# Gated y and B turned by VectorE's block transposes and a trip through DRAM instead of on TensorE

## The reference, cut to what matters

```python
proj = x @ W_in.T                       # gives xp, z, B_ssm, C_ssm, dt_low
dt = softplus(dt_low @ dt_W.T + dt_b)
scores = einsum('bcihn,bcjhn->bcijh', Cc, Bc) * Lm * dtc[:, :, None, :, :]
y_intra = einsum('bcijh,bcjhp->bcihp', scores, xc)
chunk_state = einsum('bckhn,bckhp->bchnp', Bc, wx)
...
y = (y_intra + y_cross).reshape(B, S, H, P) + xp * D_param[None, None, :, None]
y = y / rms * norm_w
y = y * silu(z)
return y @ W_out.T
```

## Time and profile before

| what | before |
|---|---|
| median of 3 runs | 2918.6 us (2917.18 to 2920.0) |
| profiled execution, its own time | 2926.86 us |
| span of the profiled execution | 2925.1 us |
| busy: PE, DVE, ACT, POOL | 95%, 70%, 59%, 50% |
| mean granted TensorE clock | 0.988 of full |

### The profile page before, as it was taken

The page is one execution under the profiler, slowest core; times in us unless marked ns, Lnnn a source line. Parts: engine busy times, 40 slices in busy tenths (PEclk is TensorE's granted clock), DMA queues, the critical chain, the costliest instruction groups (busy, mean ns, idle before and its releaser), DMA issues.

```text
span 2925.1 us, 135112 instructions
## 1 busy us (share of the span) xinstructions
PE 2769.8 (95%) x59836; PEld 2237.4 (76%) x59836; DVE 2053.4 (70%) x2871; ACT 1715.0 (59%) x3424; POOL 1463.4 (50%) x2319
## 2 busy tenths in 40 slices
PE   8999999999999999999999999999677787899998
PEld 7888888888888888888888888887566676455554
DVE  6777777777777777777777777777444443788998
ACT  5666566566666666656656656665333333666674
POOL 4666666666667667666666666666110000111111
PEclk9999999999999999999999999999899998899999
DMA  4222222222222222222222222222644443578776
GB/s 154 78 73 69 74 78 76 73 78 77 72 79 74 72 82 73 73 77 74 75 75 78 74 72 79 76 73 58 215 132 136 110 123 119 178 222 269 234 228 195
DMA packets 262711, 316.37 MB, mean 108 GB/s; under 512 B 28000, under 2 KB 184032, under 8 KB 260464
## 3 DMA queue, kind: packets, MB, share of 16 engines
q1 hardware_dynamic: 252176, 297.55, 33.7%
q10 hardware_dynamic: 9952, 10.17, 1.1%
HBM read 194.31 MB, written 113.31 MB: 105 GB/s over the span
## 4 chain that ended last, share of the span: by engine, by line
PE 89%; DVE 4%; issue 4%; DMA 1%; SPq 1%; POOL 1%; ACT 0%; ACTq 0%; DVEq 0%; POOLq 0%
PE a_proj L991 41%; PE a_mix L991 12%; PE s_ps L1714 6%; PE g_pick_ps L1465 6%; PE a_scan L1105 5%; PE s_ps L1735 4%; DVE g_picked L1394 3%; PE s_ps L1730 3%; PE a_scan L1082 3%; PE a_scan L1069 2%; PE g_acc_ps L1489 2%; PE a_mix L1057 2%; PE a_misc L1049 1%; PE a_misc L1123 1%; DMA part_dram<-res 1%
## 5 line engine op out<-in xcount | busy, mean ns | idle before, releaser
L991 PE MATMUL a_proj<-wdh,xTh 128*128 128x512 f32 x1024 | 421.2, 411 | 5.5 <-issue 3.7
L991 PE MATMUL a_proj<-wdh,xTl 128*128 128x512 f32 x1024 | 402.4, 393 | 0.3 <-issue 0.3
L991 PE MATMUL a_proj<-wdl,xTh 128*128 128x512 f32 x1024 | 400.0, 391 | 1.7 <-issue 1.7
L823 DVE COPY_PREDICATED scan_in<-mask,a_scan 64x512 f32<-64x512 uint32 x512 | 382.4, 747 | 16.1
L1671 ACT COPY s_stage<-s_ps 128x1024 f32<-128x1024 f32 x256 | 279.2, 1147 | 150.9 <-PE s_ps L1714 142.4
L464 POOL TENSOR_TENSOR dx<-xs,d_row 64x512 f32<-64x512 f32 x256 | 331.4, 1294 | 15.1
L472 POOL TENSOR_TENSOR yv<-yt,dx 128x512 f32<-128x512 f32 x128 | 189.0, 1476 | 293.2 <-DVE yt L863 293.2
L639 ACT ACTIVATE scan_in<-CT,hsel 64x128 f32<-64x128 f32 x1024 | 326.2, 388 | 4.8
L603 ACT ACTIVATE raw<-a_proj,rs 128x272 f32<-128x272 f32 x128 | 62.5, 488 | 427.4 <-PE a_proj L991 427.4
L1394 DVE COPY g_picked<-g_pick_ps 128x1024 f32<-128x1024 f32 x128 | 156.7, 1224 | 218.4 <-PE g_pick_ps L1465 218.4
L1691 DVE STREAM_TRANSPOSE s_turned<-s_stage 128x2048 f32<-128x2048 f32 x128 | 294.4, 2302 | 9.8 <-ACT s_stage L1671 9.8
(11 more groups left out here) (152 smaller groups left out, 7275.3 us busy)
## 6 DMA issues: line engine op xcount, KB each, us to landing
x<-in_x_dram SPq DMA_DIRECT2D x128, 256.0 KB, 2.7
xn_dram<-xn SPq DMA_DIRECT2D x128, 256.0 KB, 2.4
part_dram<-res SPq DMA_DIRECT2D x128, 256.0 KB, 2.5
g_xn<-xn_dram SPq DMA_DIRECT2D x512, 64.0 KB, 2.3
s_part<-part_dram SPq DMA_DIRECT2D x128, 256.0 KB, 4.1
out_dram<-s_out SPq DMA_DIRECT2D x128, 256.0 KB, 3.8
xr<-in_xT_dram SPq DMA_DIRECT2D x126, 256.0 KB, 2.9
s_inner<-inner_dram SPq DMA_DIRECT2D x32, 512.0 KB, 4.1
```

The lines of the kernel that those rows point to most:

```text
L823: nc.vector.copy_predicated(dst, mask[rows_, :].unsqueeze(1).unsqueeze(1).to_broadcast([CH, 4, 2, CH]), src).then_inc(mt_cp, 1)
L991: last = nc.tensor.matmul(out, lhs[a], rhs[c], start=(k == 0 and n == 0), stop=(k == nk - 1 and n == 2))
```

## The change

TensorE no longer turns y or B, but for the very last tile of y. DVE transposes 32x32 blocks of gated y (turn_yz) and of scaled B (turn_b) into the buffer blocks; SP stores them to DRAM and loads them back with the blocks in their new places, in four loads for four groups of 32 partitions. One store with its four loads, "even", carries y of tile n1 and B of both tiles of block s (512 KB each way); the other, "odd", carries y of tile n2+1 (256 KB each way). copy_bT, hi_yz and lo_yz read the loaded tiles in SBUF in place of PSUM. ygh and ygl get a second buffer, and the memory for all of it comes from a smaller scratch of the DMA program. Orders on ACT and the older issues of SP are kept; SP's new issues stand between them.

```diff
+    def features(n):
+        return (odd[:] if n % 2 else even[:, :, 0:KI, :]).rearrange("p b k t -> p k b t")
+    def even_part(s):
+        return slice(0 if valid(s - 1) else KI, 2 * KI if valid(s) else KI)
+    def odd_steps(s):
+        return max(0, s - 1)
...
+        def store_even(s):
+            part = even_part(s)
+            cols = slice(GRP * part.start, GRP * part.stop)
+            if valid(s):
+                sync.wait_ge(b_turned, s + 1)
+            if valid(s - 1):
+                sync.wait_ge(y_turned, 2 * s - 1)
+            sync.dma_start(keep["even"][s, :, :, cols], blocks[:, :, part, :].rearrange("p g k t -> p g (k t)")).then_inc(even_out, 16)
+        def load_even(s):
+            part = even_part(s)
+            cols = slice(GRP * part.start, GRP * part.stop)
+            sync.wait_ge(even_out, 16 * (s + 1))
+            wait(sync, yg_lo, 2 * s - 3)
+            wait(sync, bT_cp, 2 * s)
+            for g in range(4):
+                sync.dma_start(even[GRP * g:GRP * g + GRP, :, part, :].rearrange("p b k t -> p b (k t)"),
+                               even_rows[s, g][:, :, cols]).then_inc(even_in, 16)
+        def store_odd(s):
+            sync.wait_ge(y_turned, 2 * s - 2)
+            sync.dma_start(keep["odd"][s], blocks[:, :, 0:KI, :].rearrange("p g k t -> p g (k t)")).then_inc(odd_out, 16)
+        def load_odd(s):
+            sync.wait_ge(odd_out, 16 * odd_steps(s))
+            wait(sync, yg_lo, 2 * s - 4)
+            for g in range(4):
+                sync.dma_start(odd[GRP * g:GRP * g + GRP, :, :, :].rearrange("p b k t -> p b (k t)"),
+                               odd_rows[s, g]).then_inc(odd_in, 16)
         def load_x(n):
             sync.dma_start(x[:, n % (2 * STB), :], x_dram[n]).then_inc(x_in[n % (2 * STB)], 16)
                     store_xn(t, t)
             if valid(s):
                 load_rsb(s)
+            if valid(s - 2) and s < NST + 1:
+                store_odd(s)
+                load_odd(s)
             if valid(s + 1):
                 store_xn(2 * (s + 1), 0)
...
                 load_x(2 * (s + 2))
+            if s < NST + 1:
+                store_even(s)
             if valid(s + 1):
                 store_xn(2 * (s + 1) + 1, 1)
+            if s < NST + 1:
+                load_even(s)
             if valid(s - 2):
                 store_part(s - 2, 1)
...
         def copy_bT(n):
-            act.wait_ge(bT_ps, n + 1)
-            nc.scalar.copy(BT[:], misc[:, 0:HALF].rearrange("p (f t) -> p f t", f=2)).then_inc(bT_cp, 1)
+            act.wait_ge(even_in, 64 * (n // 2 + 1))
+            wait(act, sc_ps, 4 * n)
+            part = KI + 2 * (n % 2)
+            nc.scalar.copy(BT[:].rearrange("p f (b t) -> p b f t", t=GRP), even[:, :, part:part + 2, :]).then_inc(bT_cp, 1)
         def copy_x(n):
...
         def hi_yz(n):
-            act.wait_ge(yzT_ps, n + 1)
             if n == NT - 1:
+                act.wait_ge(yzT_ps, 1)
                 for i in range(2):
                     act.wait_ge(xn_out[i], 16 * NST)
-            nc.scalar.copy(gated(n)[0], turned(n)[:].rearrange("p (k t) -> p k t", k=KI)).then_inc(yg_hi, 1)
+                nc.scalar.copy(gated(n)[0], turned(n)[:].rearrange("p (k t) -> p k t", k=KI)).then_inc(yg_hi, 1)
+            else:
+                act.wait_ge((even_in, odd_in)[n % 2], 64 * (n // 2 + 2 - n % 2))
+                wait(act, o_ps, n - 1)
+                nc.scalar.copy(gated(n)[0].rearrange("p k (b t) -> p k b t", t=GRP), features(n)).then_inc(yg_hi, 1)
...
-            wait(dve, yzT_ps, n - 1)
+            wait(dve, y_turned, n - 1)
             nc.vector.tensor_tensor(yz[:, n % 2, :], yv[:], sz[:, n % 4, :], ALU.mult).then_inc(yz_cp, 1)
+        def turn_yz(n):
+            s = n // 2 + 1 + n % 2
+            wait(dve, even_out, 16 * s)
+            wait(dve, odd_out, 16 * odd_steps(s - n % 2))
+            dve.wait_ge(yz_cp, n + 1)
+            nc.vector.transpose(blocks[:, :, 0:KI, :], yz[:, n % 2, :].rearrange("p (k g l) -> p g k l", k=KI, g=4)).then_inc(y_turned, 1)
+        def turn_b(s):
+            wait(dve, even_out, 16 * s)
+            wait(dve, odd_out, 16 * odd_steps(s))
+            dve.wait_ge(scaled, 2 * s + 2)
+            for i in range(2):
+                last = nc.vector.transpose(blocks[:, :, KI + 2 * i:KI + 2 * i + 2, :],
+                                           raw[:, (2 * s + i) % 4, C_B:C_DT].rearrange("p (f g l) -> p g f l", f=2, g=4))
+            last.then_inc(b_turned, 1)
         def lo_yz(n):
             dve.wait_ge(yg_hi, n + 1)
             hi, lo = gated(n)
...
-            nc.vector.tensor_tensor(lo, turned(n)[:].rearrange("p (k t) -> p k t", k=KI), hi.bitcast(F32),
-                                    ALU.subtract).then_inc(yg_lo, 1)
+            if n == NT - 1:
+                nc.vector.tensor_tensor(lo, turned(n)[:].rearrange("p (k t) -> p k t", k=KI), hi.bitcast(F32),
+                                        ALU.subtract).then_inc(yg_lo, 1)
+            else:
+                hi, lo = [y.rearrange("p k (b t) -> p k b t", t=GRP) for y in (hi, lo)]
+                nc.vector.tensor_tensor(lo, features(n), hi.bitcast(F32), ALU.subtract).then_inc(yg_lo, 1)
         def residual(n, i):
             dve.wait_ge(o_ps, n + 1)
...
             if valid(s - 2):
+                if s < NST + 1:
+                    turn_yz(n2 + 1)
...
                 expand_c(n1 + 1)
+            if valid(s - 1):
                 gate(n1)
+                turn_yz(n1)
+            if valid(s):
+                turn_b(s)
             if valid(s + 1):
                 stats(2 * (s + 1) + 1)
                 finish_stats(2 * (s + 1) + 1)
...
+            pe.wait_ge(scaled, n + 1)
             pe.wait_ge(x_cp, n + 1)
             wait(pe, yt_cp, n)
             wait(pe, mt_cp, 4 * n)
...
             pe.wait_ge(yg_lo, n + 1)
+            if n < NT - 1:
+                wait(pe, res_cp, n)
             for k in range(KI):
                 last = split_mm(turned(n)[:], [y[:, k, :] for y in gated(n)], [w[:, k, :] for w in wo], k, KI)
...
                 project_bdt(n0 + 1)
-            if valid(s - 1):
-                transpose_b(n1)
             if valid(s):
                 project_x(n0)
-            if valid(s - 2):
-                transpose_yz(n2)
             if valid(s - 1):
                 chunk_states(n1)
                 scores(n1)
             if valid(s):
                 project_z(n0)
-            if valid(s - 1):
-                transpose_b(n1 + 1)
             if s == NST:
                 pe.wait_ge(z_cp, NT)
...
             if s == NST + 1:
                 gather["pick"](pe, 0, 1)
-            if valid(s - 2) and s < NST + 1:
...
+        even=nc.dram_tensor("even_dram", [NST + 1, P, 4, 2 * KI * GRP], F32, kind="Internal").ap(),
+        odd=nc.dram_tensor("odd_dram", [NST + 1, P, 4, KI * GRP], F32, kind="Internal").ap(),
...
-    nc = bacc.Bacc("TRN2", target_bir_lowering=False, num_devices=1)
+    nc = bacc.Bacc("TRN2", target_bir_lowering=False, num_devices=1, dynamic_dma_scratch_size=1024)
```

34 lines of the change are left out of this document (18 added, 16 removed).

## The result

The changed kernel takes 2930.26 us (median of 6 runs, 2926.18 to 2938.61); the kernel before, in the same rounds, 2919.26 (2916.31 to 2920.63). The ratio is 1.0045, 95% interval 1.0029 to 1.0061: slower by half a per cent, where a gain of 1.4% was forecast. The profiled execution has a span of 2936.8 us and a time of its own of 2938.61, the longest of the six; that of the kernel before was 8 us over its median too, so the two traces may be held against each other.

What follows compares the result with a forecast made beforehand. The prediction took PE to bound the loop. From the profiled 2926.9 us it took 62 for the loop and added 20 for the end: 2884.9, or 2877 against the median; own range 2862 to 2891, 8-in-10 range 2842 to 2925.

Steps and rivals of the forecast that it cites:

- What PE gives back: PE's transposes in a stage: removing those of y and B frees 1.48 us, 93 us over some 63 stages.
- What is late next: PE's sums wait 0.5 us for POOL's dA, held up by lo_yz; stage 30.4 us, gain 62 us over 63 stages.
- DVE: DVE in a stage: block transposes add 1.9 us, 24.9 busy of 30.4; full, but not setting the stage.
- the bound of 30.7: DVE in the loop: if each block transpose took 0.75 us, the stage would be 30.7 us.
- The round trip: Stores and loads of turned y and B: hidden in the loop, with 6 us to spare for even, 4.7 for odd.
- The end: End of the phase: turn_yz on DVE waits for the odd store behind the weight loads; a loss of 20 us.
- 2926.9 - 62 + 20: Whole kernel: profiled time less the loop's gain plus the end's loss, 2884.9, or 2876.6 against the median.
- PE alone: Rival for the loop: PE stays the only bound, POOL costs nothing; 2846 us, chance 0.18.
- the port in full: Rival at POOL: lo_yz holds it for its whole 0.65 us; gain 46 us, time 2893, chance 0.12.
- slower: Rival at POOL: block transposes hold it too, dA 1.35 us late; gain 8 us, time 2931, chance 0.14.
- the end did cost: Judges the rival that the phase's end costs nothing, store_odd getting past the weights: 2857 us, chance 0.09.
- the loads weren't late: Judges the rival that loads come over 6 us late, each us beyond costing 63 us; chance 0.05.

Runs made afterwards that it cites:

- e9: Changed kernel with lo_yz reading its second operand from PSUM instead of SBUF, low part of y left out: 2929.68 us, 1.003 of the kernel before.
- e14: Kernel before with POOL's first spread_c product of a stage issued twice, so that dA comes later: 2959.38 us, 1.0105 of the kernel before.
- e2: Changed kernel with POOL's inv_std of the next x tile moved behind step_sizes, so that dA comes earlier: 2895.68 us, 0.9918 of the kernel before.
- e1: Changed kernel with stage 64's turned-y stores and loads and result stores issued ahead of the weight loads: 2920.8 us, 0.9994 of the kernel before.
- e10: Changed kernel with the even x tile's store and the result store held back on SP until project_x(n0+1) is done: 2928.86 us, 1.0029 of the kernel before.
- e13: Changed kernel with inv_std behind step_sizes and POOL's first spread_c product of a stage issued twice: 2958.94 us, 1.0103 of the kernel before.
- e8: Changed kernel with transpose_b put back, so PE turns B and only y goes the new way: 2918.51 us, 0.9957 of the kernel before.
- e7: Kernel before with only B turned the new way, y still turned by PE: 2896.8 us, 0.9891 of the kernel before.
- e5: Changed kernel with stage 64's stores and loads ahead of the weight loads and inv_std behind step_sizes: 2884.48 us, 0.9852 of the kernel before.
- e15: Changed kernel with inv_std behind step_sizes and the first half's store_xn and store_part behind SP's wait for the second project_x: 2903.88 us, 0.9918.
- e4: Kernel before with the change's stores and loads added, read by nobody, none in stage 64; transposes stay on PE: 2926.7 us, 1.0019.
- e6: Kernel before with only its two result stores of stage 64 issued ahead of the weight loads: 2920.95 us, 0.9988 of the kernel before.
- e3: Changed kernel with 12 matmuls of 4 columns a stage added in the places of the removed transposes: 3005.79 us, 1.0286 of the kernel before.
- e12: Kernel before with only B turned the new way, stage 64's result stores ahead of the weight loads, inv_std behind step_sizes: 2872.66 us, 0.9842.
- e11: Kernel before with only POOL's inv_std moved behind step_sizes: 0.9983 of the kernel before, 5 us.

## Why the prediction was wrong, point by point

The time was forecast at 2877 and came out at 2930, above its range.

*What PE gives back*: 1.48 us a stage forecast, 1.32 measured. B's pairs gave 0.22 each. Of 0.52 for a set of y's, 0.44 came: the 0.31 from the last matmul to chunk_states holds 0.08 that 0.23 between plain matmuls didn't show. I took the distance from the first transpose to the next work, and forgot that the next work's first start behind a large matmul has a price of its own.

*What is late next*: right in mechanism, and in size partly by luck. The wait at the sums was forecast at 0.5 us and is 0.58 in the mean of 62. The hold lies where it was put, on the row ahead of dA, and is 0.32 us for 0.4; but mv also comes from DVE 0.22 us later, which the forecast had at nothing. The Trainium skill, SBUF — State Buffer, section "Who interferes with whom", has a DVE instruction with two SBUF inputs exclude one of GpSimd that reads SBUF. The trace agrees for lo_yz (nm 502 ns, 193 in e9). Not foreseen were 0.10 us between the start of the sums and project_x (1.49 for 1.39; e14, which only adds a wait, has 1.49 too) and 0.08 a stage in the mean for chunk_states. 1.32 - 0.58 - 0.10 - 0.08 = 0.56, and the usual stage came down by 0.47; the last 0.1 is not accounted for. It is some 30 us over the loop for 62.

*DVE*: turn_yz takes 0.71 us (0.6 taken, bound 0.75) and turn_b 0.73 (0.7). "DVE is full but doesn't set the stage" held for the change in that PE waits for POOL's dA and not for DVE, though a part of dA's lateness is DVE's, as just said. It did set it in e2, at 30.72, so the bound of 30.7 that I gave for slow transposes became the floor as soon as dA was early.

*The round trip*: hidden in the loop, as worked out. The page's DMA part has the even store at 2.6 us and part_dram's at 3.3 (2.5 before):

```profile
part_dram<-res SPq DMA_DIRECT2D x128, 256.0 KB, 3.3
...
even_dram<-blocks SPq DMA_DIRECT2D x63, 512.0 KB, 2.6
```

No wait of ACT for even or odd is among those between 300 and 1900 us.

*The end*: a loss of 20 us forecast, 16.3 measured; turn_yz waited 23.40 us for odd_dram's store. Right.

*The step that failed* is in the sum: "2926.9 - 62 + 20". Both of its sides missed. The 62 us are 35 too many: the usual stage gives 0.47 us and not 0.98, 27 us over 58 stages, by the pieces just listed. And it has no term for PE's pauses, which the earlier trace rows hide, since the stretch with 596.6 of 600 us busy has only two of them, 1.84 and 0.92 us: in the stages from the sixth on the excess grew by 22 us, and the first stages lost 2. The end was 4 too dear, and what lies behind it 1 shorter. 35 + 22 + 2 - 4 - 1 is the 54 us between forecast and profiled time. The mis-sized gain alone would have left the time at some 2908, still faster and in the range; the pauses made it slower.

*What lengthens the pauses.* Each pause follows an instruction packet by 2.2 to 3.3 us, with busy DMA engines or idle ones. Over all traces the length goes with how long dA is ready before PE starts the sums, rather than with whether PE waits for it. These are the pauses of over 0.8 us between 300 and 1900 us in which PE ran dry in the scan behind the sums or just after it (within 2.1 us of the sums' start). Where PE waits for dA, 0.05 us from its end to the sums' start remain:

```text
end of dA ahead of the sums' start, us        number of pauses and their length, us
0.05, PE waits    after                       7    2.11 to 2.86
                  e1                          7    2.12 to 2.88
                  e9                          7    1.83 to 2.99
                  e10                         7    1.61 to 2.60
                  e14                         3    2.30 to 3.00
                  e13, six stages             6    1.77 to 2.44
0.05 to 0.15      e8, PE barely waits         8    1.01 to 2.88
0.38, no wait     e7                          3    2.70 to 2.77
0.66 to 0.86      e2, e5, e15                21    1.29 to 2.05
0.85              e13, the seventh stage      1    1.48
0.91 to 0.92      before, e4, e6             18    0.82 to 2.19
1.36              e3                          3    0.86 to 1.71
1.65              e12                         2    0.97
2.2               e11                         3    1.03 to 1.28
```

Moving dA changes them in both directions: moving inv_std shortens them in the changed kernel (e2), in the kernel before (e11) and with B alone (e12 against e7, which differ otherwise only in SP's orders of stage 64); the doubled product lengthens them (e13, e14). Moving the stores does little where PE waits (e10) and nothing in e15. So a dA that comes close to its use costs twice where PE waits for it, in each stage and once more in each seventh, and in e7 it costs pauses alone. Not shown: why PE's packet comes later when dA is late just ahead of the scan; when a packet is asked for stands in no view. e8 has both long and short pauses with dA at the same distance, so this isn't all. That the long ones come every seventh stage now goes with the number of PE's instructions in a stage, since e2, with the same stream, has its pauses at the same places; how the packets' borders line up with the stages wasn't tried. e4's traffic, with no wait for dA, made the three pauses 0.24 us shorter, 0.46 longer and 0.23 longer, which is no more than e6 shows without it, so what the traffic does there is open.

*Rivals*: "PE alone" was wrong by POOL and DVE; "the port in full" came nearest with 0.73 us of stage gained for 0.47; "slower" gave the right time by the wrong way, since in the stage shown dA is later by 0.46 us against project_bdt, 0.29 of it in POOL's operations and 0.17 because DVE is later, and not by the 1.25 of that rival; the end did cost; the loads weren't late.

## What to carry to other kernels

Before counting an engine's freed instructions as time, look for the pauses of that engine without a cause: sum the stages' excess over the median stage, and treat it as a term of its own, that grew here from 17 to 39 us when an input of the work just ahead of a burst of small instructions came 0.9 us later against PE, and that can grow without any wait to show for it. Take off the bound engine only as much as the next two engines in line can follow; here a third of the edit (B, four of the twelve transposes) gave as short a usual stage as all of it, with none of the end's loss. And when work is added to a queue, its last iterations need an order of their own ahead of the next phase's bulk loads.

## What the runs showed of the hardware

Pauses of PE of 2 to 3 us were mostly followed by a granted clock of 0.50 for three to five us (33 of 48 in the 17 traces between 300 and 1900 us), and those of 0.8 to 1.5 us never (0 of 56); of those between, 7 of 32 were. The length alone doesn't decide: after 2.58 us at 1548.81 in the changed kernel the clock stayed full (excess 2.48), after 1.76 us at 1298.46 in e15 it fell, and in the kernel before one pause of 1.86 us had an excess of 3.68 and one of 1.84 of 1.80. A fall costs about as much as the pause: 5.15 us of excess for 2.86 of pause.

An fp32 matmul of 4 columns is dearer for PE than a transpose of 128. The 12 of e3 are 24 records a stage, and they cost about 2.2 us, 0.18 for a matmul. Four of them, as eight records, ahead of chunk_states:

```profile
1012.29 0.95 PE L1178 MATMUL a_mix<-wmat,mean 128*128 128x4 f32 x8
1013.17 0.65 PE L1156 MATMUL a_scan<-xs,raw 64*32 64x64 f32 x32
```

That is 0.88 us from start to start, 0.22 for each, where four transposes took 0.52, 0.13 for each.

A store of 256 KB that is issued behind the weights' loads lands some 17.7 us later (issued at 2054.65, its loads at 2072.40) in place of 3.2, the median of the 63 such stores.
